# Graph network with two residual layers: one tile's sums over edges gathered by transfers instead of multiplied, in steps two to twelve

## The chip, the cores and the metric

One core of a Trainium2 chip runs the whole program. The metric is the device time of one execution in microseconds; a time given for a kernel is the median of its runs.

## What is computed

A graph of 3125 nodes with 128 features and 53125 edges `(src, dst)`, sorted by `dst`, among them a loop at each node. Two residual layers; the first has twelve steps:

```python
def L0(h, src, dst):                     # h = relu(layernorm(x))
    h = tanh(h @ W_in + b_in)
    deg = clip(segment_sum(1, dst), 1)[:, None]
    for _ in range(12):
        agg = segment_sum(h[src], dst) / deg
        h = h + (tanh(gelu(agg @ W1 + b1) @ W2 + b2) - relu(clearance) * h) * 0.5
    return h
x = x + L0(relu(layernorm(x)), src, dst)
x = x + L1(relu(layernorm(x)), src, dst) # two GCN convolutions, loops added, normed by degree
```

In the reference's inputs no node of the tail tile (below) has more than 26 edges.

## The kernel before

**Sums over edges as products.** The kernel builds the adjacency matrix of counts, `adj`, once in SBUF as f16 (25 tiles of source nodes by 3125 destination nodes). Each step, the sum over edges is a product of TensorE: `edge_sums` multiplies, for a group of destination nodes, all 25 tiles of the state with their part of `adj`. The f32 state is split into two f16 parts, `hi` (made on ScalarE) and `lo` (made on VectorE), so that a group takes 49 products (the short last tile holds both parts in one).

**Groups.** The 25 tiles of destination nodes form seven groups, `GROUPS`: five of four tiles (512 columns), a sixth, g = 5, of 437 columns (tiles 21 to 24) and the tail, g = 6, of the one tile 20 (nodes 2560 to 2687, 128 columns). For a group PE's order in `step` is `edge_sums(g)`, `outputs(g - 2)`, `hidden(g - 1)`; behind the tail come `hidden(6)`, the first 16 products of the next step's group 0, `outputs(5)` and `outputs(6)`. `hidden` is the product with W1, `outputs` the product with W2 (one f32 product for each tile and each half of the hidden row, so eight for four tiles). VectorE has `means` (division by the degree), `add_bias`, `update` (the new state) and `lo` of the next step; ScalarE has `gelu`, `tanh` and `hi` of the next step. ScalarE starts on `hi` for the next step when the tail's sums are done, since these are the last that read the old parts. Each engine works through its own queue in the order written; semaphores hold them together. Step one, `first_step`, has its own order, steps two to eleven are a loop, and step twelve has the next layer's first work mixed in (`last_step`: `add_loops`, `add_input`, `row_factors`, `norm_rows`).

**Entry.** SyncE (SP) loads the edges; VectorE finds for windows of five destination nodes where their edges start (`thresholds`, `past`, `here`, then `start_i`), and GpSimd (POOL) fetches each window's edges by five indirect transfers (L524). Then 52 batches of windows are turned into columns of `adj`: VectorE makes one-hot rows (L1168), TensorE multiplies them (L611), ScalarE copies the result (L913). Between the batches stands the entry product: GpSimd scales the rows of x to the layer norm's (L530, 25 tiles), and TensorE transposes and multiplies them. `degrees` and a flag check that all edges were found (`missed`); with the flag set, a general path would be taken, which these inputs don't take. GpSimd has nothing to do after the entry, and the DMA little until step twelve.

Of the kernel before, what the change touches and what calls it, by code (L numbers as in the profile page):

```python
# [28 lines left out]
NODES = 3125  # L29
# [23 lines left out]
LAST_HEAD = GROUP_TILES  # L53

# [35 lines left out]
ROW_BOUND = 12.0  # L90


def gnn_kernel(nc, x, src, dst, W_in, b_in, W1, b1, W2, b2, clearance, G1, gb1, G2, gb2, out):
    ctx = ExitStack()
    with ctx:
# [12 lines left out]
        x2_dram = nc.dram_tensor("x2_scratch", (NODES, FEAT), F32).ap()  # L108
        rest_dram = nc.dram_tensor("rest_scratch", (TILES, P, NODES), F16).ap()
# [16 lines left out]
        cols = sb("cols", [128, 300], F32)  # L126
        flag = sb("flag", [1, 1], I32)
        scratch = sb("scratch", [128, SCRATCH], F32)
# [18 lines left out]
        now_unscale = col(1)  # L147
        next_scale = col(1)
        top = col(4)
# [4 lines left out]
        deg = col(TILES)  # L154
        rdeg = col(TILES)
        root = col(TILES)
        dinv = col(TILES)
        assert at[0] <= 300
        spare = cols[:, at[0] - 4 * TILES:at[0]]
        stats2 = spare[:, 0:12 * 6].rearrange("p (k s) -> p k s", s=6)  # L160
        guess = spare[:, 12 * 6:12 * 6 + TILES]
# [14 lines left out]
        assert o + 512 == SCRATCH  # L176

# [20 lines left out]
        term_rest = [late[0:terms, 9, c:c + FEAT] for c in range(1302, 1302 + 2 * FEAT, FEAT)]  # L198
        yT = [late[:, 4 * i:4 * i + 4, 1302:1302 + P] for i in range(2)]
# [36 lines left out]
        thresholds = place(WINDOWS)  # L236
        past = place(WINDOWS)
        here = place(WINDOWS)
# [14 lines left out]
        row_i = place(WINDOWS, talli)  # L253
        ones16 = place(1, tall).bitcast(F16)
# [47 lines left out]
        s_y = sem("entry_rows_ready")  # L302
        s_yT = sem("entry_rows_transposed")
# [34 lines left out]
        s_xr = [sem(f"x_reloaded{g}") for g in range(NG)]  # L338
# [3 lines left out]
        s_x2o = [sem(f"x2_stored{g}") for g in range(NG)]  # L342
# [23 lines left out]
        s_res = sem("result_stored")  # L366

# [21 lines left out]
        def _(sp):  # L389
# [21 lines left out]
            def store_norms(done):  # L411
                sp.dma_start(window_layout(rdeg_dram), rdeg[0:WQ, :].rearrange("p (g d) -> p g d", g=WCOLS)
                             ).then_inc(done, 16)
                sp.dma_start(window_layout(dinv_dram), dinv[0:WQ, :].rearrange("p (g d) -> p g d", g=WCOLS)
                             ).then_inc(done, 16)
# [7 lines left out]

            sp.wait_ge(s_norms, 1)
            store_norms(s_norms_out)
# [5 lines left out]
            with sp.If(missed != 0):  # L431
# [14 lines left out]
                sp.dma_start(deg[0:WQ, :].rearrange("p (g d) -> p g d", g=WCOLS), window_layout(deg_dram)  # L446
# [4 lines left out]
                store_norms(g_normso)  # L451
# [6 lines left out]


            for g in range(NG + 2):  # L460
                if g < NG:
                    sp.wait_ge(s_aggT, (STEPS - 1) * NG + g + 1 + OPEN)
                    for sbuf, dram in rows(xload, x, g):
                        sp.dma_start(sbuf, dram).then_inc(s_xr[g], 16)
                if g >= 2:
# [3 lines left out]
                    for sbuf, dram in rows(state, x2_dram, b):  # L469
                        sp.dma_start(dram, sbuf).then_inc(s_x2o[b], 16)  # L470
# [14 lines left out]
        def _(pool):  # L485
# [3 lines left out]
            nc.gpsimd.iota(thresholds, pattern=[[WIN, WINDOWS]], base=0, channel_multiplier=0, **big)  # L489
            nc.gpsimd.iota(chunk_d[:, CHUNK + 1:CHUNK + 2], pattern=[[0, 1]], base=0, channel_multiplier=CHUNK, **big)  # L490
            nc.gpsimd.iota(wfirst, pattern=[[WQ * WIN, WCOLS]], base=0, channel_multiplier=WIN, **big).then_inc(s_const, 1)
# [30 lines left out]
            for g in range(WCOLS):  # L522
                pool.wait_ge(s_start, g + 1)
                nc.gpsimd.indirect_dma_start(  # L524
                    wedge_i[:, g, :], None, packed_dram.rearrange("(n o) -> n o", o=1),
                    bass.IndirectOffsetOnAxis(ap=start_i[:, g:g + 1], axis=0)).then_inc(s_wedges[g], 16)
            pool.wait_ge(s_ln, 1)
            for g, (k0, nt) in enumerate(GROUPS):
                for k in range(k0, k0 + nt):
# [4 lines left out]
            missed = pool.value_load(flag[0:1, 0:1], min_val=0, max_val=1)  # L534
            with pool.If(missed != 0):
# [3 lines left out]

                def stream_rest(turn, g):  # L540
                    c0, n = SPANS[g]
                    with pool.Fori(0, TILES) as k:
                        pool.wait_ge(s_restu, (turn * NG + g) * TILES + k + OPEN)
                        pool.dma_start(rest_tile[:, 0:n],
                                       rest_dram[bass.ds(k, 1), :, c0:c0 + n].rearrange("k p d -> p (k d)")
                                       ).then_inc(s_rest[g], 16)

                with pool.Fori(0, STEPS + 2) as t:
# [5 lines left out]
        def _(pe):  # L554
# [4 lines left out]
            for g in range(WCOLS):  # L559
                nc.tensor.matmul(ps[0:WQ, g, 0:CHUNK + 2], here[:, g * WQ:(g + 1) * WQ], chunk_d, start=True, stop=True  # L560
                                 ).then_inc(s_chunk, 1)
            pe.wait_ge(s_ident, 2)
# [12 lines left out]
            def degree_total():  # L575
                pe.wait_ge(s_deg, 1)
                nc.tensor.matmul(ps[0:1, 7, 64:65], deg_sum[0:WQ, :], ones_col[0:WQ, :], start=True, stop=True
                                 ).then_inc(s_degsum, 1)


            def entry_transpose(g):
                k0, nt = GROUPS[g]
                pe.wait_ge(s_y, g + 1)
# [156 lines left out]

            pe.wait_ge(s_last[2], 1)
# [20 lines left out]
            def step(t, last):  # L762
                for g in range(NG):
                    if g == 0:
                        edge_sums(t, 0, (s_hi, s_lo), t * NG, (HEAD, TILES)).then_inc(s_agg, 1)
                    else:
                        pe.wait_ge(s_aggT, t * NG + g - 1 + OPEN)
                        edge_sums(t, g, (s_hi, s_lo), t * NG).then_inc(s_agg, 1)
                    if g >= 2:
                        outputs(t, g - 2)  # L770
                    if g >= 1:
# [82 lines left out]
        def _(act):  # L854
# [43 lines left out]

            def entry_copy(g):
# [19 lines left out]
            for b in range(ENTRY_BATCHES):  # L919
# [6 lines left out]
                if b - 1 in PROD_AT:  # L926
                    entry_tanh(PROD_AT.index(b - 1))
                    split_hi(PROD_AT.index(b - 1), PROD_AT.index(b - 1) + 1, first_scale)
            with act.Fori(ENTRY_BATCHES // 2, BATCHES // 2) as i:
# [99 lines left out]
        def _(dve):  # L1029
# [43 lines left out]

            for g in range(WCOLS):
# [6 lines left out]
                                ).then_inc(s_start, 1)  # L1081

# [42 lines left out]
            def degrees():  # L1125
# [4 lines left out]
                                     root[0:WQ, :].rearrange("p (g d) -> p g d", d=WIN), ALU.subtract))  # L1130
                V.tensor_reduce(deg_sum[0:WQ, :], deg[0:WQ, :], AX.X, ALU.add).then_inc(s_deg, 1)
# [45 lines left out]
            for b in range(ENTRY_BATCHES):  # L1177
# [8 lines left out]
                if b == 6:  # L1186
# [3 lines left out]
                    link(V.tensor_copy(total[0:1, :], ps[0:1, 7, 64:65]))  # L1190
                    V.tensor_scalar(flag[0:1, 0:1], total[0:1, :], float(EDGES), None, ALU.not_equal).then_inc(s_flag, 1)
# [10 lines left out]
            with dve.If(missed != 0):  # L1202
# [57 lines left out]
                half_, y_ = root[0:WQ, :], dinv[0:WQ, :]  # L1260
                then(V.tensor_scalar(rdeg[0:WQ, :], deg[0:WQ, :], 1.0, None, ALU.max))
                then(V.reciprocal(rdeg[0:WQ, :], rdeg[0:WQ, :]))
                then(V.tensor_scalar(deg[0:WQ, :], deg[0:WQ, :], 1.0, None, ALU.add))
                then(V.tensor_scalar(half_.bitcast(I32), deg[0:WQ, :].bitcast(I32), 1, None, ALU.arith_shift_right))
                then(V.tensor_scalar(y_.bitcast(I32), half_.bitcast(I32), -1.0, float(0x5F3759DF), ALU.mult, ALU.add))
                for _ in range(4):
                    then(V.tensor_tensor(half_, y_, y_, ALU.mult))
                    then(V.scalar_tensor_tensor(out=half_, in0=half_, scalar=-0.5, in1=deg[0:WQ, :], op0=ALU.mult,
# [5 lines left out]

            dve.wait_ge(s_last[2], 1)
# [6 lines left out]
            def means(t, g, first=False):  # L1282
# [4 lines left out]
                source = ps[:, FIRST_BANK[g], :] if first else ps_agg[2 if g == TAIL else g % 2]  # L1287
# [289 lines left out]
```

## Time and profile before

| | us |
|---|---|
| runs | 1301.18, 1301.23, 1305.0; median 1301.23 |
| the profiled execution | 1300.27 |
| its span | 1298.5 |
| TensorE busy | 1255.0 |
| VectorE / ScalarE / GpSimd busy | 400.9 / 298.3 / 64.4 |

The span is what the profile's records cover; the time of the execution lies 1.77 us above it. All rows below count from the span's start. The entry takes until some 132 us, step one until some 202 us, steps two to twelve some 86.6 us each, and the second layer the rest. The granted clock of TensorE is 1.00 in the steps, which is the 2.4 GHz level.

### The profile page before, as it was taken

How to read it: one execution, taken by the hardware profiler on the slowest of the kernel's cores; microseconds unless marked ns; L12 is line 12 of the kernel's file. 1: busy time of each engine (PE TensorE's matmuls, PEld its weight loads, DVE VectorE, ACT ScalarE, POOL GpSimd, SP SyncE). 2: the span in 40 equal slices, each digit the busy share in tenths (PEclk: the TensorE clock that was granted, in tenths of full speed). 3: DMA queues.
4: the chain of work that ended last, by engine and by line, in shares of the span. 5: the costliest groups of instructions: out<-in, count | busy, mean ns of one | idle time of the engine just before them, and what ended most of it. 6: DMA issues, size and time to landing. Idle time of an engine off the chain costs nothing.

```text
span 1298.5 us, 17275 instructions
## 1 busy us (share of the span) xinstructions
PE 1255.0 (97%) x7194; PEld 707.0 (54%) x7194; DVE 400.9 (31%) x817; ACT 298.3 (23%) x438; POOL 64.4 (5%) x56
## 2 busy tenths in 40 slices
PE   3888999999999999999999999999999999999998
PEld 1766465564565645645656456456564564565545
DVE  7999122131131221311312213113122132382312
ACT  1898221131121211311212113112121131120100
POOL 4940000000000000000000000000000000000000
PEclk7899999999999999999999999999999999999999
DMA  3000200000000000000000000000000000220101
GB/s 100 3 1 2 63 1 1 1 1 0 0 0 0 0 0 0 0 0 0 0 0 0 0 0 0 0 0 0 0 0 0 0 1 24 66 61 1 50 17 34
DMA packets 24552, 13.77 MB, mean 11 GB/s; under 512 B 6173, under 2 KB 23609, under 8 KB 24388
## 3 DMA queue, kind: packets, MB, share of 16 engines
q1 hardware_dynamic: 22334, 11.88, 3.4%
q10 hardware_dynamic: 1782, 1.06, 0.3%
q8 instruction: 26, 0.43, 0.1%
q0 software_dynamic: 400, 0.33, 0.1%
q14 instruction: 10, 0.08, 0.0%
HBM read 9.42 MB, written 3.44 MB: 10 GB/s over the span
## 4 chain that ended last, share of the span: by engine, by line
PE 88%; DVE 8%; issue 2%; DMA 1%; ACT 0%; DVEq 0%; SPq 0%; POOL 0%; ACTq 0%; POOLq 0%
PE ps L715 63%; PE ps L757 10%; PE ps L748 9%; DVE scratch L1168 5%; PE ps L628 3%; PE ps L829 1%; DVE lo L1151 1%; DMA adj<-packed_scratch,adj 1%; PE ps L611 0%; PE ps L571 0%; DVE cols L1367 0%; DMA adj<-in_dst_dram 0%; DVE state L1394 0%; PE ps L565 0%; DVE ps L1295 0%
## 5 line engine op out<-in xcount | busy, mean ns | idle before, releaser
L715 PE MATMUL ps<-adj,hi 128*128 128x512 f16 (+2 forms) x2275 | 747.2, 352 | 1.3 <-DVE lo L1151 1.3
L715 PE MATMUL ps<-adj,lo 128*128 128x512 f16 (+2 forms) x2184 | 730.4, 351 | 0.0
L715 PEld LDWEIGHTS ps<-adj,hi 128*128 128x128 f16 x2275 | 220.8, 97 | 228.0 <-issue 14.5
L715 PEld LDWEIGHTS ps<-adj,lo 128*128 128x128 f16 x2184 | 212.4, 97 | 224.1 <-issue 18.2
L1295 DVE TENSOR_TENSOR ps<-ps,bias 128x512 f32<-128x512 f32 (+1 forms) x84 | 53.9, 641 | 532.4 <-PE ps L757 532.4
L955 ACT ACTIVATE scratch<-ps 128x512 f32<-128x512 f32 (+1 forms) x84 | 46.3, 552 | 614.7 <-DVE ps L1295 614.6
L946 ACT ACTIVATE scratch<-ps,b1c,cols 128x512 f32<-128x512 f32 (+2 forms) x168 | 111.9, 724 | 170.7 <-PE ps L748 169.9
L757 PEld LDWEIGHTS ps<-w,scratch 128*128 128x128 f32 x1200 | 144.2, 192 | 8.1
L757 PE MATMUL ps<-w,scratch 128*128 128x128 f32 x1200 | 146.1, 275 | 0.0
L748 PE MATMUL ps<-scratch,w 128*128 128x512 f32 (+2 forms) x336 | 137.8, 538 | 0.0
L1288 DVE TENSOR_TENSOR scratch<-ps,scratch 128x512 f32<-128x512 f32 (+2 forms) x84 | 51.9, 619 | 178.7 <-PE ps L748 131.3
L1168 DVE TENSOR_TENSOR scratch<-scratch 128x1536 f16<-128x1536 f16 (+1 forms) x106 | 92.2, 940 | 0.5 <-PE ps L611 0.5
L913 ACT ACTIVATE adj<-ps 128x1500 f16<-128x1500 f32 (+1 forms) x52 | 76.0, 1480 | 14.9 <-PE ps L611 14.6
L748 PEld LDWEIGHTS ps<-scratch,w 128*128 128x128 f32 x336 | 57.3, 191 | 38.9 <-issue 37.2
L1300 DVE SCALAR_TENSOR_TENSOR state<-state,cols,scratch 128x512 f32<-128x512 f32 (+1 forms) x84 | 58.3, 694 | 47.0 <-ACT scratch L955 46.7
L611 PE MATMUL ps<-scratch 128*128 128x125 f16 x625 | 55.4, 249 | 13.2 <-DVE scratch L1168 11.9
L1151 DVE SCALAR_TENSOR_TENSOR lo<-state,cols,hi 128x512 f16<-128x512 f32 (+2 forms) x91 | 59.9, 672 | 13.6 <-ACT hi L857 12.8
L611 PEld LDWEIGHTS ps<-scratch 128*128 128x128 f16 x625 | 45.8, 110 | 29.0 <-DVE scratch L1168 25.7
L628 PE MATMUL ps<-adj,hi 128*128 128x512 f16 (+2 forms) x175 | 58.8, 353 | 1.6 <-ACT adj L933 1.6
L628 PE MATMUL ps<-adj,lo 128*128 128x512 f16 (+2 forms) x168 | 56.6, 352 | 0.0
L857 ACT ACTIVATE hi<-state,cols 128x512 f16<-128x512 f32 (+1 forms) x84 | 52.1, 669 | 19.4 <-PE ps L715 17.3
L530 POOL TENSOR_SCALAR state<-state,cols 128x128 f32<-128x128 f32 x25 | 49.2, 1981 | 11.4 <-DVE cols L1139 11.4
(143 smaller groups left out, 247.7 us busy)
## 6 DMA issues: line engine op xcount, KB each, us to landing
scratch<-rdeg_scratch SPq DMA_DIRECT2D x1, 1562.5 KB, 8.8
state<-in_x_dram SPq DMA_DIRECT2D x5, 256.0 KB, 3.7
scratch<-in_x_dram SPq DMA_DIRECT2D x5, 256.0 KB, 2.7
x_scratch<-state SPq DMA_DIRECT2D x5, 256.0 KB, 2.7
scratch<-dinv_scratch SPq DMA_DIRECT2D x5, 256.0 KB, 3.9
state<-x_scratch SPq DMA_DIRECT2D x5, 256.0 KB, 3.1
out_dram<-state SPq DMA_DIRECT2D x5, 256.0 KB
adj<-adj ACTq DMA_DIRECT2D x1, 390.6 KB, 9.1
```

The source lines that it names most:

```text
L611: return nc.tensor.matmul(target[:, :, place * WIN:(place + 1) * WIN], Lb[buf][:, b, :, i_], Rb[buf][:, b, :, i_].rearrange("p (k d) -> p ...
L628: mm = nc.tensor.matmul(ps[:, FIRST_BANK[g], 0:n], values[:, k, :], adj[:, k, c0:c0 + n], start=(at == 0 and values is hi), stop=(k == SHORT))
L715: return nc.tensor.matmul(bank, values[:, k, :], adj[:, k, c0:c0 + n], start=is_first, stop=is_last)
L748: nc.tensor.matmul(ps_hid_tail[h] if g == TAIL else ps_hid[h][:, 0:n], w1[:, h * FEAT:(h + 1) * FEAT], agg[g == TAIL][:, 0:n], start=True, ...
L757: mm = nc.tensor.matmul(ps_out[g == TAIL][:, i * FEAT:(i + 1) * FEAT], hid[g == TAIL][:, h, i * P:(i + 1) * P], w2[:, h, :], start=(h == 0 ...
L857: nc.scalar.activation(tiles_of(hi, group), tiles_of(state, group), ACT.Copy, scale=factor).then_inc(s_hi, 1)
L913: nc.scalar.activation(adj[:, :, bass.ds((i * 2 + u) * BATCH * WIN, BATCH * WIN)].rearrange("p k (b c) -> p b k c", b=BANKS), ps[:, 3 * u: ...
L946: nc.scalar.activation(hid[g == TAIL][:, h, 0:n], ps_hid_tail[h] if g == TAIL else ps_hid[h][:, 0:n], ACT.Gelu, bias=b1c[:, h:h + 1], scal ...
L1151: return V.scalar_tensor_tensor(out=lo[:, k0:k1, :], in0=values[:, k0:k1, :], scalar=0.0 if factor is None else factor, in1=hi[:, k0:k1, : ...
L1168: last_ = V.tensor_tensor(buf[:, 0:b, :, 0:w], c_.broadcast_to((128, b, m, w)), k_.broadcast_to((128, b, m, w)), ALU.is_equal)
L1295: V.tensor_tensor(p_, p_, bias_of(1, nt), ALU.add).then_inc(s_bias, 1)
L1300: V.scalar_tensor_tensor(out=tiles_of(state, g), in0=tiles_of(state, g), scalar=now_keep, in1=act_out[:, 0:n_], op0=ALU.mult, op1=ALU.add) ...
```

## The change

**The tail's sums.** In steps two to twelve the sums over edges of the tail tile are no longer multiplied. After each step, SP stores the new f32 state to `state_dram` (3125 rows and a row of zeros). GpSimd then gathers: for c = 0 to 31, one indirect transfer brings to each of 128 partitions the row of the c-th edge of its node, or the row of zeros where the node has fewer edges. Three tiles in SBUF take them in turn (`tail_sum`, rooms that are free in the steps): the first transfer to a tile overwrites, the others add (`compute_op`), and each waits until the one before it into the same tile has landed. TensorE adds the three by products with the identity (`tail_sums`), which also transposes. As these sums are of unscaled rows, `means` multiplies the tail by a scale of the step.

**The list of rows.** `tail_rows` (128x32) comes from one more search in the entry: 128 more columns in `thresholds`, `past` and `here`, one more product, four operations on VectorE, one more indirect transfer, and five small operations on GpSimd. If a node had more than 32 edges, or others were missing, all rows would point to the zeros and the old products would run.

**The order in group g = 5.** Its sums are cut at place 15 (`SPLIT`); `hidden(4)` and `outputs(3)` stand between the two parts, in this order.

**Rows of x.** The first two groups (eight tiles) are scaled on ScalarE instead of GpSimd. The small degree vectors move from `cols` to room in `adj`; `s_xr` and `s_x2o` are merged into other semaphores.

```diff
+ACT_ROWS = 2
+
+CAP = 32
+TAIL_NODE = GROUPS[TAIL][0] * P
+PLACES = 3
+PLACE_TURNS = [len(range(i, CAP, PLACES)) for i in range(PLACES)]
...
+        tail_sum = [w_in[:, :], bias[:, 0, :], hid[1][:, 0, :]][0:PLACES]
...
-        thresholds = place(WINDOWS)
-        past = place(WINDOWS)
-        here = place(WINDOWS)
+        thresholds = place(WINDOWS + P)
+        past = place(WINDOWS + P)
+        here = place(WINDOWS + P)
...
+            def store_state(t):
+                for g in range(NG):
+                    sp.wait_ge(s_upd, t * NG + g + 1)
+                    for sbuf, dram in rows(state, state_dram, g):
+                        sp.dma_start(dram, sbuf).then_inc(s_st[g], 16)
+
+            store_state(1)
+            with sp.Fori(2, STEPS) as t:
+                for i in range(PLACES):
+                    sp.wait_ge(s_place[i], t * (16 * PLACE_TURNS[i]) - 16 * PLACE_TURNS[i])
+                store_state(t)
...
+            pool.wait_ge(s_start, WCOLS + 1)
+            nc.gpsimd.indirect_dma_start(
+                tail_rows[:, :], None, packed_dram.rearrange("(n o) -> n o", o=1),
+                bass.IndirectOffsetOnAxis(ap=tail_start, axis=0)).then_inc(s_tedge, 16)
+            nc.gpsimd.memset(tail_block[:, 0:WIN], 0.0)
+            pool.wait_ge(s_tedge, 16)
+            nc.gpsimd.tensor_scalar(tail_f, tail_rows[:, :], tail_base, None, ALU.subtract).then_inc(s_tc2, 1)
+            pool.wait_ge(s_tc2, 1)
...
+                if g < ACT_ROWS:
+                    continue
...
+            pool.wait_ge(s_mrow, 1)
+            nc.gpsimd.tensor_scalar(tail_rows[:, :], tail_f, missing_row, None, ALU.max).then_inc(s_trow, 1)
...
+            def gather_tail(t):
+                for g in range(NG):
+                    pool.wait_ge(s_st[g], t * (16 * parts(g)))
+                for c in range(CAP):
+                    i, turn = c % PLACES, c // PLACES
+                    before = (t - 1) * PLACE_TURNS[i] + turn
+                    if before:
+                        pool.wait_ge(s_place[i], 16 * before)
+                    nc.gpsimd.indirect_dma_start(
+                        tail_sum[i], None, state_dram, bass.IndirectOffsetOnAxis(ap=tail_rows[:, c:c + 1], axis=0),
+                        compute_op=ALU.bypass if turn == 0 else ALU.add).then_inc(s_place[i], 16)
...
+            for t in range(1, STEPS):
+                gather_tail(t)
+                with pool.If(missed != 0):
+                    for g in range(NG):
+                        stream_rest(t, g)
...
+            def tail_sums(t):
+                bank = ps_agg[2][:, 0:P]
+
+                def place(i):
+                    pe.wait_ge(s_place[i], t * (16 * PLACE_TURNS[i]))
+                    return nc.tensor.matmul(bank, tail_sum[i], ident[:, :], start=(i == 0), stop=(i == PLACES - 1))
+
+                for i in range(PLACES - 1):
+                    place(i)
+                with pe.If(missed != 0):
+                    for k in range(TILES):
+                        c0, n = SPANS[TAIL]
+                        nc.tensor.matmul(bank, hi[:, k, :], adj[:, k, c0:c0 + n], start=False, stop=False)
+                        if k != SHORT:
+                            nc.tensor.matmul(bank, lo[:, k, :], adj[:, k, c0:c0 + n], start=False, stop=False)
+                    with pe.Fori(0, TILES) as r:
+                        add_rest(t, TAIL, bank, r)
+                return place(PLACES - 1)
...
+                        if g == TAIL:
+                            tail_sums(t).then_inc(s_agg, 1)
+                        elif g == TAIL - 1:
+                            edge_sums(t, g, (s_hi, s_lo), t * NG, (0, SPLIT))
+                            hidden(t, g - 1)
+                            outputs(t, g - 2)
+                            edge_sums(t, g, (s_hi, s_lo), t * NG, (SPLIT, TILES)).then_inc(s_agg, 1)
+                        else:
+                            edge_sums(t, g, (s_hi, s_lo), t * NG).then_inc(s_agg, 1)
+                    if g >= 2 and g != TAIL - 1:
                         outputs(t, g - 2)
-                    if g >= 1:
+                    if g >= 1 and g != TAIL - 1:
...
+            act.wait_ge(s_ln, 1)
+            for g in range(ACT_ROWS):
+                k0, nt = GROUPS[g]
+                for k in range(k0, k0 + nt):
+                    last = nc.scalar.activation(state[:, k, :], state[:, k, :], ACT.Identity, bias=ln_b[:, k:k + 1],
+                                                scale=ln_a[:, k:k + 1])
+                last.then_inc(s_ya, 1)
...
+            V.tensor_scalar(tail_base, tail_first, float(PACK), None, ALU.mult)
...
+            dve.wait_ge(s_chunk, WCOLS + 1)
+            link(V.tensor_scalar(tail_junk, ps[:, WCOLS, 0:CHUNK], tail_first, 0.0, ALU.is_lt, ALU.add,
+                                 accum_out=tail_found))
+            link(V.tensor_scalar(tail_start_f, tail_found, ps[:, WCOLS, CHUNK + 1:CHUNK + 2], 0.0, ALU.add, ALU.max))
+            V.tensor_scalar(tail_start, tail_start_f, float(EDGES - CAP), None, ALU.min).then_inc(s_start, 1)
...
+                V.tensor_tensor(tail_block[0:WQ, 0:WIN], deg[0:WQ, w0:w0 + WIN], tail_mask, ALU.mult)
...
-                    link(V.tensor_copy(total[0:1, :], ps[0:1, 7, 64:65]))
-                    V.tensor_scalar(flag[0:1, 0:1], total[0:1, :], float(EDGES), None, ALU.not_equal).then_inc(s_flag, 1)
+                    V.tensor_scalar(total, ps[:, 7, 64:65], float(EDGES), None, ALU.not_equal)
+                    link(V.tensor_reduce(missing, ps[:, 7, 96:96 + WIN + CAP], AX.X, ALU.add))
+                    link(V.scalar_tensor_tensor(out=missing, in0=missing, scalar=0.0, in1=total, op0=ALU.not_equal,
+                                                op1=ALU.max))
+                    V.tensor_scalar(flag[0:1, 0:1], missing[0:1, :], 0.0, None, ALU.add).then_inc(s_flag, 1)
+                    V.tensor_scalar(missing_row, missing, float(NODES), None, ALU.mult).then_inc(s_mrow, 1)
...
+                if g == TAIL and not first:
+                    V.scalar_tensor_tensor(out=agg[1], in0=source[:, 0:n_], scalar=now_tail, in1=row[:, c0:c0 + n_],
+                                           op0=ALU.mult, op1=ALU.mult).then_inc(s_aggT, 1)
+                    return
...
+                if not isinstance(t, int) or t > 0:
+                    dve.wait_ge(s_st[g], t * (16 * parts(g)))
...
+                V.tensor_scalar(now_tail, tail_scale[:, bass.ds(t, 1)], 1.0, None, ALU.mult)
```

## Rows read from the trace of the kernel before

**Rows 1.** The page, part 1: busy time, share, instructions.

```profile
PE 1255.0 (97%) x7194; PEld 707.0 (54%) x7194; DVE 400.9 (31%) x817; ACT 298.3 (23%) x438; POOL 64.4 (5%) x56
```

**Rows 2.** The chain that ended last, 345 to 378 us: start, us, what.

```profile
349.81 9.09 PE ps L715 x49
358.90 1.78 PE ps L757 x16
360.68 1.72 PE ps L748 x4
362.40 2.76 PE ps L715 x49
365.16 1.84 PE ps L757 x16
367.00 1.91 PE ps L748 x8
368.92 3.46 PE ps L715 x16
```

**Rows 3.** The same chain over the whole span.

```profile
12.84 7.36 DMA adj<-packed_scratch,adj
...
448.97 2.76 PE ps L715 x49
...
1128.91 9.08 PE ps L715 x49
...
1167.90 4.05 PE ps L715 x18
```

**Rows 4.** POOL's instructions in order of time, 12 to 20 us.

```profile
14.55 1.21 POOL L524 DMA_INDIRECT adj<-packed_scratch,adj  x1 [0.31 <-issue]
16.06 1.21 POOL L524 DMA_INDIRECT adj<-packed_scratch,adj  x1 [0.30 <-issue]
```

**Rows 5.** One line's instructions, L524: landing.

```profile
DMA to landing us min/median/max: 3.1/3.4/3.6
```

**Rows 6.** DVE in order of time, 374 to 378 us.

```profile
376.95 0.35 DVE L1300 SCALAR_TENSOR_TENSOR state<-state,cols,scratch 128x128 f32<-128x128 f32 x1 [0.42 <-ACT scratch L955]
```

**Rows 7.** One line's instructions, L470: SP's stores of x2 rows.

```profile
L470 SPq DMA_DIRECT2D x_scratch<-state x8: 320/364/374, 1103.0 to 1161.7; - x8
...
DMA to landing us min/median/max: 1.6/2.6/3.9
```

**Rows 8.** All engines in order of time, 360.6 to 363.5 us.

```profile
360.72 0.70 DVE L1295 TENSOR_TENSOR ps<-ps,bias 128x512 f32<-128x512 f32 x1 [9.79 <-PE ps L757]
...
362.03 1.44 ACT L946 ACTIVATE scratch<-ps,b1c,cols 128x512 f32<-128x512 f32 x2
...
362.83 0.61 DVE L1288 TENSOR_TENSOR scratch<-ps,scratch 128x437 f32<-128x437 f32 x1
```

**Rows 9.** Windows: busy us by engine, PEclk, DMA share, GB/s.

```profile
12.00:20.00 8.00, 3.23 (x7) 1.25 (x5) 5.53 (x24) 1.49 (x2) 5.94 (x5) 0.84 0.90 220
30.00:82.00 52.00, 44.98 (x432) 37.30 (x433) 51.32 (x73) 43.68 (x42) 49.18 (x25) 0.89 0.06 2
380.00:449.00 69.00, 69.00 (x342) 35.62 (x340) 8.51 (x13) 8.26 (x13) 0.00 (x0) 1.00 0.00 0
```

(The engines stand in the order PE, PEld, DVE, ACT, POOL.)

**Rows 10.** Groups by line and form: busy us, mean ns, idle before.

```profile
L530 POOL TENSOR_SCALAR state<-state,cols 128x128 f32<-128x128 f32 x25 | 49.2, 1981 | 11.4 <-DVE cols L1139 11.4
...
L955 ACT ACTIVATE scratch<-ps 128x128 f32<-128x128 f32 x12 | 3.3, 278 | 15.7 <-DVE ps L1295 15.7
...
L1312 DVE TENSOR_SCALAR cols<-cols 128x1 f32 x10 | 1.5, 154 | 0.0
```

**Rows 11.** DVE in order of time, 4 to 21 us.

```profile
7.94 0.87 DVE L1052 SCALAR_TENSOR_TENSOR adj<-adj 125x625 f32<-125x625 f32 x1
...
20.22 0.29 DVE L1100 TENSOR_SCALAR adj<-adj 125x128 f32<-125x128 int32 x1 [1.98 <-DMA adj<-packed_scratch,adj]
```

**Rows 12.** DVE in order of time, 1138 to 1142 us.

```profile
1141.85 0.61 DVE L1288 TENSOR_TENSOR scratch<-ps,scratch 128x437 f32<-128x437 f32 x1
```

More of the change, by code:

```diff
@@ L53 @@
 LAST_HEAD = GROUP_TILES
+SPLIT = TILES - 10
 WIN = 5
@@ L147, in gnn_kernel @@
         now_unscale = col(1)
+        missing = col(1)
+        missing_row = col(1)
+        now_tail = col(1)
         next_scale = col(1)
+        tail_scale = bound
         top = col(4)
@@ L153, in gnn_kernel @@
         dinv_col = col(TILES)
[L154 to L161, printed above, removed]
+        guess = col(TILES)
+        stats2 = col(GROUP_TILES * 6).rearrange("p (k s) -> p k s", s=6)
+        assert at[0] <= 252
         row = scratch[:, 0:NODES]
@@ L198, in gnn_kernel @@
         term_rest = [late[0:terms, 9, c:c + FEAT] for c in range(1302, 1302 + 2 * FEAT, FEAT)]
+        deg, rdeg, root, dinv = (late[:, 7, 1440 + i * TILES:1440 + (i + 1) * TILES] for i in range(4))
+        general_deg, general_rdeg, general_root, general_dinv = (act_out[0:WQ, i * TILES:(i + 1) * TILES]
+                                                                 for i in range(4))
+        tail_f, tail_neg, tail_block = (late[:, 4, 1440:1440 + CAP], late[:, 5, 1440:1440 + CAP],
+                                        late[:, 6, 1440:1440 + WIN + CAP])
+        tail_mask = late[0:WQ, 6, 1500:1500 + WIN]
         yT = [late[:, 4 * i:4 * i + 4, 1302:1302 + P] for i in range(2)]
@@ L253, in gnn_kernel @@
         row_i = place(WINDOWS, talli)
+        tail_first, tail_base, tail_found, tail_start_f = (place(1, tall) for _ in range(4))
+        tail_start = place(1, talli)
+        tail_junk = place(CHUNK, tall)
         ones16 = place(1, tall).bitcast(F16)
@@ L366, in gnn_kernel @@
         s_res = sem("result_stored")
+        s_zero = sem("zero_row_stored")
+        s_tedge = sem("tail_edges_loaded")
+        s_tc2 = sem("tail_rows_chain")
+        s_tmask = sem("tail_mask_ready")
+        s_mrow = sem("missing_row_ready")
+        s_trow = sem("tail_rows_ready")
+        s_tab2 = sem("tail_scales_ready")
+        s_place = [sem(f"tail_rows_added{i}") for i in range(PLACES)]
+        s_st = [sem(f"state_stored{g}") for g in range(NG)]
         block = ctx.enter_context(nc.Block())
@@ L538, in _ @@
                 pool.wait_ge(g_pair, 16)
[L540 to L548, printed above, removed]
+                for g in range(NG):
+                    stream_rest(0, g)
+            pool.wait_ge(s_trow, 1)
+            pool.wait_ge(s_zero, 16)
+            for t in range(1, STEPS):
+                gather_tail(t)
+                with pool.If(missed != 0):
+                    for g in range(NG):
+                        stream_rest(t, g)
+            with pool.If(missed != 0):
+                with pool.Fori(STEPS, STEPS + 2) as t:
                     for g in range(NG):
@@ L561, in _ @@
                                  ).then_inc(s_chunk, 1)
+            nc.tensor.matmul(ps[:, WCOLS, 0:CHUNK + 2], here[:, WINDOWS:], chunk_d, start=True, stop=True
+                             ).then_inc(s_chunk, 1)
             pe.wait_ge(s_ident, 2)
@@ L1267, in _ @@
                     then(V.tensor_tensor(half_, y_, y_, ALU.mult))
-                    then(V.scalar_tensor_tensor(out=half_, in0=half_, scalar=-0.5, in1=deg[0:WQ, :], op0=ALU.mult,
+                    then(V.scalar_tensor_tensor(out=half_, in0=half_, scalar=-0.5, in1=general_deg, op0=ALU.mult,
                                                 op1=ALU.mult))
@@ L1358, in add_input @@
                 dve.wait_ge(s_upd, STEPS * NG + g + 1)
-                dve.wait_ge(s_xr[g], 16 * parts(g))
+                dve.wait_ge(s_x[g], 2 * 16 * parts(g))
                 if k1 < k0 + nt:
```

94 lines of the change are left out of this document (69 added, 25 removed).

## The prediction, made before the changed kernel ran

> **What bounds the kernel now.** I read the page first: TensorE is busy for 1255.0 of 1298.5 us [rows 1]. Then the chain that ended last, over one step of the loop. Its pieces touch each other and all belong to PE [rows 2], and the same place of the next step, the sums of the tail, comes 448.97 - 362.40 = 86.57 us later [rows 2, 3]. So a step costs what PE has to do in it, and PE's work that is taken out comes out of the time, unless something else becomes late. The reader is to see in [rows 2]: the sixth group's sums (x49, 9.09 us), the outputs of group 3 (1.78), the hidden product of group 4 (1.72), the tail's sums (x49, 2.76), the outputs of group 4 (1.84), the hidden products of groups 5 and 6 (1.91), then the next step's first sums. Outside the steps, the entry stage is another kernel: there DVE is busy for 51.32 of 52 us [rows 9]. In the last step DVE takes over too: from 1141.85 us [rows 12] the chain runs over it until the next layer's sums start at 1167.90 [rows 3].
>
> **The tail's sums, the term that pays.** Steps two to twelve lose 49 products of 128 columns, 2.76 us each time [rows 2]. In their place stand three f32 products of 128x128 with the identity. An outputs turn has eight such products, shows as 16 records and takes 1.78 us [rows 2], so three are 6 records x 0.111 = 0.67 us. Saving per step 2.76 - 0.67 = 2.09 us. The branch on the flag was inside the tail's sums before and stays; formerly 49 short products hid it, now two do. I take 0 for it and keep up to 0.5 us a step for the range (the whole new group is 0.67).
>
> **The order in the sixth group.** 30 of its 49 products (15 tiles) run first, then hidden(4), outputs(3), then 19 products, the tail, outputs(4). Nothing is added on PE; the question is only whether outputs(4) finds gelu(4) done. In the trace of before outputs(3) ends at 360.68, the bias starts at 360.72, and after it and tanh the two gelus run from 362.03 to 363.47 [rows 2, 8]: 2.79 us after the outputs. After the change PE has 19 x 9.09/49 = 3.52 plus 0.67 = 4.19 us between. Covered, with 1.4 us to spare; had hidden(4) and outputs(3) stayed behind the sums, only 1.72 + 0.67 us would lie there and each step would stall by about 0.4 us. means(5) (0.61 us [rows 8]) has the tail's 0.67 and outputs(4)'s 1.78 us as cover before hidden(5). After the tail everything stands as before, since the high parts of the next step wait for the tail's sums in both kernels. So I count 2.09 us in a step of the loop.
>
> **The gather, which has to be hidden.** A step's gather is 32 indirect transfers of 128 rows of 512 B on POOL, in three accumulators; a transfer waits for the landing of the one three before it. It starts when the new state lies in DRAM. The last update ends at 376.95 + 0.35 = 377.30 [rows 6]; SP then issues the last store (0.36 us), and eight like it land after 1.6 to 3.9, median 2.6 us [rows 7]. That is 379.3 to 381.6, by the median 380.3; as the last one is a single tile, I take 380.0. PE comes to the tail at 448.97 [rows 3], no later after the change than before, counted from there. Cover: 69.0 us.
> The nearest rows are the five indirect loads of window edges, 125 rows of 512 B: 16.06 - 14.55 = 1.51 us from issue to issue, and 3.1 to 3.6 us from issue to landing; the first took 7.36 us until it was used, beside a DMA that moved 220 GB/s [rows 3 to 5, 9]. By issue the gather takes 31 x 1.51 + 3.4 = 50.2 us. By landing it takes 11 rounds of 3.4 = 37.4 us. Neither row adds to its destination. An adding one must read the sum first; if that costs as much again as the shortest landing of a store, a round is 3.4 + 1.6 = 5.0 us, 55.0 us in all. I take 50 to 55, hidden by 14 us or more, so its price on PE is 0. Bounds of a round: 3.1 below and 7.36 above.
> If the gather takes G, a step is G + (86.57 - 2.09 - 69.0) = G + 15.5 us. It starts to cost at G = 69.0 (a round of 6.27 us, or an issue every 2.12) and is slower than before from G = 71.1, a round of 6.46 us.
> DVE and POOL can hinder one another: POOL's row scaling took 1981 ns for a 128x128 tile while DVE had no pause [rows 9, 10], and DVE is busy for 8.51 us between 380 and 449 [rows 9]. Were every one of them lost to POOL, G would be 59 to 64, still covered.
> [...]
>
> **Queues.** SP gets 8 stores a step, 88 in all, and waits for the former gather before it stores the next state; behind that wait stand only stores, and x's reloads in the last step, which wait for the first means of that step anyway. update() newly waits for the store of the former state, some 20 us older than its place. POOL has nothing else to do in the steps. One more tiny DVE operation in step_scales (0.15 us [rows 10]) falls into DVE's idle time.
>
> **The last step.** There DVE is the bound. means(5) starts at 1141.85 in before [rows 12], after the update of group 3. After the change the sixth group ends at 1128.91 [rows 3] + 12.59 (9.09, 1.78 and 1.72) = 1141.50, and means(5) can start some 0.2 later, at 1141.70. DVE's chain behind it is unchanged, so this step gives 0.15 us, not 2.09.
>
> **Entry.** x's first two groups go to ACT: eight tiles at 278 ns (the row of a 128x128 tanh [rows 10]) = 2.2 us, and ACT is busy for 43.68 of 52 us there [rows 9], so 0. POOL's 25 tiles fill 49.2 us [rows 10], the 17 left over 33.7; the chain holds none of them, so nothing is won either. DVE, the bound, gets more: `past` and `here` grow from 625 to 753 columns (0.87 us [rows 11] x 0.20, twice: 0.35), and five small operations come in (tail_base, one product in degrees(), three at the flag) at 0.15 us [rows 10], some 0.2 with their waits, another 1.0: about 1.3 us. The search of the tail's edges, four operations as for each window group, falls into the 1.98 us for which DVE waits for the first window edges [rows 11], and so may part of the first terms. I take +1.0, bounds 0 and 3.
>
> **Sum.** 10 x 2.09 + 0.15 = 21.05 off, 1.0 on: 20.05. The profiled execution took 1300.27 us, so 1280.2. The median of the runs lies 0.96 above it: 1281.2, forecast **1281 us**.
>
> **Rivals.**
> *The gather comes late* (slower, one mechanism: an adding round on POOL is longer than 6.46 us). For it: no row shows an adding transfer, one traced transfer took 7.36 us, and twice the 3.4 would be 6.8. Against it: the 7.36 was beside some 220 GB/s of loads, and in the steps the DMA is idle [rows 9]. Price: with 6.8 us, G = 74.8, a step 90.3, 3.7 us more than now, x11 = 41: about 1343 us. With 7.36, G = 81.0, a step 96.5: about 1411. Were the issue to double to 3.0 us (twice as many descriptors), G = 96: about 1570. Chance 0.16 for slower, and 0.03 that it falls between 6.3 and 6.5 us and there is no change.
> *PE stalls at the small tail group* (branch, three waits, gelu late): up to 0.8 us a step, 8 us in all, 1285 to 1290. For it: three products hide little. Against it: 1.4 us spare in the hand-over. Chance 0.12.
> *The whole gain is hidden, because DVE or ACT sets the step*: against it, DVE and ACT are busy 8.51 and 8.26 of 69 us [rows 9]. Chance 0.01.
> *The change doesn't do what it says*: if a node of the tail had over 32 edges, the rows would all point to the zero row and the old sums would run again. In the reference's inputs its nodes have at most 26. Chance under 0.01.
> *The forecast*: chance 0.68, own range 1277 to 1286.
>
> **Numbers that follow.** Faster 0.80, same 0.04, slower 0.16; 0.3% (4 us) is about what a measurement of this kernel can tell from no change. The range takes the forecast and the stall: from 1275 (all eleven steps at 2.09 and nothing for the entry is 1278, less 3 for what the rows can't resolve) to 1294 (0.5 us a step for the branch, 3 for the entry, and the start of a late gather). What is left out is the late gather.
>
> **What would show it.** Tail group on PE: 6 records, 0.67 us, step 84.5 us, no PE idle before it: right. A wait of PE for a DMA into w_in, bias or hid at the tail: late gather. 352 adding transfers on POOL, their distance 1.5 to 1.7 us and last landing 50 to 55 us after the first: right; distance above 2.1: wrong. outputs(4) waiting for ACT: the stall. In the last step means(5) moves by under 0.3 us relative to its group's start. The first step's sums start 1 us later than before.

## The result, and the profile after

The changed kernel takes 1280.6 us (median of four runs, 1279.38 to 1281.51) against 1301.2 before: ratio 0.984, interval 0.9828 to 0.9852, some 20.6 us less. The forecast was 1281 us, range 1275 to 1294.

The chain that ended last, over the same step of the changed kernel (start, us, what). L819 are the sums over edges, L871 hidden, L880 outputs, L850 the three products with the identity:

```profile
348.89 5.56 PE ps L819 x30
354.46 1.72 PE ps L871 x4
356.17 1.78 PE ps L880 x16
357.96 3.52 PE ps L819 x19
361.48 0.67 PE ps L850 x6
362.15 1.79 PE ps L880 x16
363.94 1.91 PE ps L871 x8
365.85 3.46 PE ps L819 x16
```

Beside [rows 2]: the 2.76 us of the tail are 0.67, in six records, and nothing stands between the pieces. The outputs behind them come again at 446.57 (whole chain), 84.42 us after 362.15; a step took 86.57. From that whole chain, the places where the other parts show:

```profile
133.27 14.67 PE ps L732 x67
...
446.57 1.79 PE ps L880 x16
...
1108.67 5.56 PE ps L819 x30
...
1147.40 4.05 PE ps L819 x18
```

From the sixth group to the next layer's sums the last step takes 38.73 us, 38.99 before [rows 3]: it gains 0.26. The first step's sums start at 133.27; before, at 132.04 by the same chain. The balance of the span: 10 x 2.15 = 21.5 and 0.26 off, 1.23 on, 20.5; the span went from 1298.5 to 1278.1, by 20.4.

The gather (L627), POOL in order of time in that step (each bracket: idle before, and what ended it):

```profile
293.67 1.00 POOL L627 DMA_INDIRECT w_in<-state_scratch,tail_rows  x1 [27.18 <-DMA state_scratch<-state]
294.97 0.96 POOL L627 DMA_INDIRECT bias<-state_scratch,tail_rows  x1 [0.30 <-issue]
...
297.50 1.57 POOL L627 DMA_INDIRECT w_in<-state_scratch,tail_rows  x1 [0.30 <-issue]
299.37 1.55 POOL L627 DMA_INDIRECT bias<-state_scratch,tail_rows  x1 [0.31 <-issue]
...
349.43 1.55 POOL L627 DMA_INDIRECT bias<-state_scratch,tail_rows  x1 [0.31 <-issue]
```

Three overwriting transfers at 1.25 to 1.30 us apart, then adding ones at 1.85, and in this step never a wait for a landing: POOL's issue sets the pace. The last one is issued at 349.43, 55.8 us after the first; PE comes to the tail at 361.48. The cover is 361.48 - 293.67 = 67.8 us. Ten of the eleven gathers take 55.7 to 56.1 us from first to last issue. The last one takes 57.5 us, with the only two waits for a landing (1.17 and 0.30 us).

### The profile page after: what moved, and what is told of

Read it like the earlier page. It is cut to its first block, busy times and chain, and to the rows that moved or that the text cites. A ratio compares the mean times of both kernels' runs of the same rounds, so it can differ in the third digit from the quotient of the medians.

```text
span 1278.1 us, 17094 instructions
## 1 busy us (share of the span) xinstructions
PE 1234.4 (97%) x6725; PEld 688.0 (54%) x6725; DVE 406.4 (32%) x840; ACT 301.1 (24%) x446; POOL 572.4 (45%) x413
## 4 chain that ended last, share of the span: by engine, by line
PE 88%; DVE 7%; issue 2%; DMA 1%; ACT 1%; DVEq 0%; SPq 0%; POOL 0%; ACTq 0%; POOLq 0%
PE ps L819 62%; PE ps L880 10%; PE ps L871 10%; DVE scratch L1319 4%; PE ps L732 3%; PE ps L960 1%; PE ps L715 1%; PE ps L850 1%; DMA adj<-packed_scratch,adj 1%; DVE lo L1302 0%; PE ps L670 0%; DMA adj<-in_dst_dram 0%; DVE adj L1188 0%; DVE state L1560 0%; PE ps L664 0%
## 5 line engine op out<-in xcount | busy, mean ns | idle before, releaser
L819 PE MATMUL ps<-adj,hi 128*128 128x512 f16 (+2 forms) x2000 | 715.7, 370 | 2.0 <-DVE lo L1302 2.0
L819 PE MATMUL ps<-adj,lo 128*128 128x512 f16 (+2 forms) x1920 | 698.9, 370 | 0.0
L627 POOL DMA_INDIRECT w_in<-state_scratch,tail_rows x121 | 181.9, 1504 | 455.0 <-DMA state_scratch<-state 393.0
L819 PEld LDWEIGHTS ps<-adj,hi 128*128 128x128 f16 x2000 | 194.6, 97 | 225.1 <-issue 12.6
L819 PEld LDWEIGHTS ps<-adj,lo 128*128 128x128 f16 x1920 | 186.7, 97 | 219.6 <-issue 14.6
L627 POOL DMA_INDIRECT bias<-state_scratch,tail_rows x121 | 181.6, 1501 | 37.8 <-issue 36.6
L627 POOL DMA_INDIRECT scratch<-state_scratch,tail_rows x110 | 164.0, 1491 | 33.6 <-issue 33.3
L880 PEld LDWEIGHTS ps<-w,scratch 128*128 128x128 f32 x1200 | 144.2, 192 | 13.3 <-issue 5.3
L880 PE MATMUL ps<-w,scratch 128*128 128x128 f32 x1200 | 145.7, 275 | 0.6 <-ACT scratch L1087 0.6
L871 PE MATMUL ps<-scratch,w 128*128 128x512 f32 (+2 forms) x336 | 138.0, 538 | 0.0
L1449 DVE TENSOR_TENSOR scratch<-ps,scratch 128x512 f32<-128x512 f32 (+2 forms) x73 | 48.8, 670 | 172.4 <-PE ps L871 131.3
L871 PEld LDWEIGHTS ps<-scratch,w 128*128 128x128 f32 x336 | 58.0, 190 | 40.3 <-issue 36.9
L732 PE MATMUL ps<-adj,hi 128*128 128x512 f16 (+2 forms) x175 | 58.8, 353 | 1.6 <-ACT adj L1074 1.6
```

The costliest lines, as they stand in the source:

```text
L627: nc.gpsimd.indirect_dma_start(tail_sum[i], None, state_dram, bass.IndirectOffsetOnAxis(ap=tail_rows[:, c:c + 1], axis=0), compute_op=ALU. ...
L732: mm = nc.tensor.matmul(ps[:, FIRST_BANK[g], 0:n], values[:, k, :], adj[:, k, c0:c0 + n], start=(at == 0 and values is hi), stop=(k == SHORT))
L819: return nc.tensor.matmul(bank, values[:, k, :], adj[:, k, c0:c0 + n], start=is_first, stop=is_last)
L871: nc.tensor.matmul(ps_hid_tail[h] if g == TAIL else ps_hid[h][:, 0:n], w1[:, h * FEAT:(h + 1) * FEAT], agg[g == TAIL][:, 0:n], start=True, ...
L880: mm = nc.tensor.matmul(ps_out[g == TAIL][:, i * FEAT:(i + 1) * FEAT], hid[g == TAIL][:, h, i * P:(i + 1) * P], w2[:, h, :], start=(h == 0 ...
```

## The experiments

All are edits of the changed kernel but e2, which is an edit of the one before. Times are medians; e4 and e12 are single executions.

**e1, the old order in the sixth group.**

```diff
-                        elif g == TAIL - 1:
-                            edge_sums(t, g, (s_hi, s_lo), t * NG, (0, SPLIT))
-                            hidden(t, g - 1)
-                            outputs(t, g - 2)
-                            edge_sums(t, g, (s_hi, s_lo), t * NG, (SPLIT, TILES)).then_inc(s_agg, 1)
...
-                    if g >= 2 and g != TAIL - 1:
+                    if g >= 2:
...
-                    if g >= 1 and g != TAIL - 1:
+                    if g >= 1:
```

> The changed kernel with the sixth group's sums in one piece again (sums, outputs of group 3, hidden product of group 4, tail, outputs of group 4). Theory: only the hidden product (1.72) and the small tail group (0.67) lie between the outputs of group 3 and those of group 4, and gelu of group 4 is done 2.79 us after the former, so PE waits 0.4 us a step for ACT; step 84.8 instead of 84.42, about 1285 us. Rival (the cut does nothing): 1280.6 us, no wait of the outputs' matmuls on ACT.

1289.2 us, ratio 0.9907 (0.9892 to 0.9922); a step takes 85.22 us (452.68 to 537.90 in its chain). All engines in order of time, behind the tail:

```profile
447.22 1.44 ACT L1082 ACTIVATE scratch<-ps,b1c,cols 128x512 f32<-128x512 f32 x2
...
447.78 0.39 PE L850 MATMUL ps<-ident,scratch 128*128 128x128 f32 x2
...
448.71 2.05 PE L880 MATMUL ps<-w,scratch 128*128 128x128 f32 x16 [0.54 <-ACT scratch L1082]
```

L1082 is gelu here. PE waits 0.54 us for it, and the same outputs then take 2.05 us instead of 1.79, another 0.26. The granted clock stays 1.00 in the steps, so the clock is not the reason. Their first weight load starts with them at 448.71, while in the changed kernel it starts 0.11 us ahead of the products (361.88 and 361.99); that this makes the 0.26 is not shown. The theory stands, its price was half of the measured 0.80 us a step.

**e2, the new order without the gather.** The same cut in the kernel before.

> The kernel before with only the new order in the sixth group. Theory: there the tail's 2.76 us already cover gelu of group 4, so nothing is to be had: step 86.57, 1301 us, within 0.3 us in the last step. Rival (the order gives a part of the gain by itself): step below 86.4, 1299 us or less.

1301.1 us, ratio 0.9996 (0.9987 to 1.0005). The cut is worth nothing by itself; once the tail is short it keeps 8.6 of the 20.6 us (1289.2 against 1280.6).

**e3, both: gather and products.** (`means` also divides the tail as before; that line is left out here.)

```diff
-                for i in range(PLACES - 1):
-                    place(i)
...
-                return place(PLACES - 1)
+                for i in range(PLACES):
+                    pe.wait_ge(s_place[i], t * (16 * PLACE_TURNS[i]))
+                return edge_sums(t, TAIL, (s_hi, s_lo), t * NG)
```

> The changed kernel with all stores and gathers running, but the tail's sums multiplied as before from the f16 parts; the gathered rows are waited for and not used. Theory: gather and stores cost PE nothing, all the gain is in the replaced products; step 86.5, and the entry's 1.2 us on top of before: 1302 to 1303 us. Rival (44 GB/s of traffic and POOL's 48 us a step slow DVE, ACT or PE somewhere): step above 86.8, over 1305 us.

1303.0 us, ratio 1.0008 (0.9999 to 1.0017); the sums of group 0 come at 456.65 and 543.22, a step of 86.57 us as before. 88 stores and 352 indirect transfers (11 gathers of 32) cost the step nothing that shows. So the gain is the replaced products, with the order that lets them count (e1).

**e4, one accumulator** (`PLACES = 1`).

> PLACES 1: all 32 transfers of a step go into one accumulator, each waits for the landing of the one before. A step is then the gather plus 16.6 us, so its length gives the round of an adding transfer, which no row shows. Theory (round 5.0 us, the value taken in the prediction): step 177 us, about 2300 us. Rival, landing as in the loads of before (3.4): step 125, about 1730 us. Rival, twice that (6.8): step 234, about 2930 us.

1940 us. POOL in order of time, two transfers late in one gather and one early in the next:

```profile
306.67 1.55 POOL L627 DMA_INDIRECT w_in<-state_scratch,tail_rows  x1 [2.89 <-DMA w_in<-state_scratch,tail_rows]
311.08 1.55 POOL L627 DMA_INDIRECT w_in<-state_scratch,tail_rows  x1 [2.87 <-DMA w_in<-state_scratch,tail_rows]
...
362.56 1.56 POOL L627 DMA_INDIRECT w_in<-state_scratch,tail_rows  x1 [2.00 <-DMA w_in<-state_scratch,tail_rows]
```

A round of adding takes 4.41 us late in a gather (311.08 - 306.67), of which the transfer is 4.15 in the chain, and 3.5 us early in one. The mean over the eleven gathers is 3.93 us, between the 3.4 of the loads and the 5.0 that the prediction took. POOL's part of an adding transfer is 1.55 us from the first to the last of them, by median. The wait behind it is 2.0 us until the 14th transfer, rises until about the 25th and stays at 2.9 (medians by place). From the 27th on all 128 partitions take the row of zeros, since no node has more than 26 edges, and before that more and more of them do. That reading one row so often slows the landing would fit, but no run here isolates it.

**e12, one accumulator and no adding** (`compute_op=ALU.bypass` for all; the tail's sums are left out, only the last row arrives).

> PLACES 1 as in e4, but no transfer adds, all 32 overwrite (the sums of the tail are left out: only the last row arrives). e4 gave 4.15 us from issue to landing and 1.55 us on POOL for an adding transfer. Theory (adding costs POOL 0.6 us in making the descriptors and nothing behind it): on POOL 0.95 us, landing 3.5 to 3.6 us, about 1750 us. Rival (the read of the destination also takes time behind POOL): landing under 3.3 us, under 1700 us. Rival (adding costs nothing but issue overlaps): landing 4.1 as in e4, 1930 us.

1703 us. The same view, again late and early:

```profile
304.64 0.94 POOL L627 DMA_INDIRECT w_in<-state_scratch,tail_rows  x1 [2.99 <-DMA w_in<-state_scratch,tail_rows]
308.52 0.94 POOL L627 DMA_INDIRECT w_in<-state_scratch,tail_rows  x1 [2.93 <-DMA w_in<-state_scratch,tail_rows]
...
339.48 0.94 POOL L627 DMA_INDIRECT w_in<-state_scratch,tail_rows  x1 [1.83 <-DMA w_in<-state_scratch,tail_rows]
```

0.94 us on POOL instead of 1.55. The wait behind it is 2.9 us in both late in a gather, 1.8 against 2.0 early, and 2.30 against 2.40 in the mean. So adding costs 0.68 us a round (3.93 against 3.25 in the mean): 0.6 on POOL and 0.1 behind it. The theory stands for that split. Its 1750 us came out too high because it took e4's 4.15, a landing late in a gather, for every transfer; that the total came near the 1700 of the rival with time behind POOL is luck, since that time is only 0.1 us.

**e5, two accumulators** (`PLACES = 2`).

> PLACES 2: 16 rounds in two accumulators. Issue alone takes 31 x 1.85 = 57 us, which 67.8 us cover. Theory: it stays hidden if a round is below (67.8 - 2) / 16 = about 4.2 us, then 1281 us; with a round of 5.0 the gather takes 80 us, a step 96.6, about 1415 us. Between, the time rises by 16 x 11 = 176 us for each us of round above 4.2.

1280.9 us, ratio 0.9849 (0.9834 to 0.9864). Two issues take 3.7 us, more than a round early in a gather (3.5) and less than one late in it (4.4), so POOL now waits in the later half; in the same step the transfers start from 292.55 to 354.93, 62.4 us instead of 55.8, and with a landing of 4.15 the gather ends 1.3 us before PE's 360.35. Two would have done, but only just.

**e6 and e7, 36 and 40 transfers a step** (`CAP`).

> CAP 36: four more transfers a step, 36 in all. By issue 35 x 1.85 - 3 x 0.55 = 63.1 us, plus a landing of 3 to 5 us: 66 to 68, just under the 67.8 us of cover. Theory (bound by POOL's issue): 1281 us, up to 4 us more. Rival (landings set the pace, and the gather is nearer to its cover than the issue shows): 1290 us and more.

> CAP 40: by issue 39 x 1.85 - 3 x 0.55 = 70.5 us plus 3 to 5 us of landing, so 74 to 75.5, over the cover by 6 to 8 us; a step is gather + 16.6 = 90.5 to 92.1. Theory: 1348 to 1366 us, with PE waiting before the tail. Rival (something else than the tail's wait follows the gather, or it has more cover than counted): under 1330.

CAP 36: 1280.1 us, ratio 0.9839 (0.9824 to 0.9854); the last issue is at 356.88, its landing by e4's 4.15 at 361.0, and PE reaches the tail at 361.55. CAP 40: 1385.8 us, ratio 1.0646 (1.063 to 1.0662). The whole loss comes with four more transfers. In its chain:

```profile
468.94 4.41 DMA w_in<-state_scratch,tail_rows
473.39 1.65 PE ps L850 x6
475.04 2.69 PE ps L880 x16
477.74 1.91 PE ps L871 x8
```

The gather starts at 398.39 and ends at 473.35, 75.0 us, as worked out. The step is 473.39 - 378.65 = 94.7 us and not 91.6. Its windows (length, busy us of PE, PEld, DVE, ACT, POOL, then PEclk, DMA share, GB/s) say why:

```profile
360.00:370.00 10.00, 10.00 (x57) 6.03 (x55) 1.17 (x3) 1.06 (x3) 8.48 (x6) 1.00 0.30 36
370.70:378.60 7.90, 1.01 (x6) 0.32 (x4) 0.61 (x1) 0.37 (x1) 4.64 (x3) 0.74 0.30 34
378.65:386.10 7.45, 7.45 (x31) 6.43 (x32) 3.44 (x6) 4.16 (x7) 0.00 (x0) 0.60 0.51 141
```

The products of the tail in PE's rows, with the wait before them:

```profile
378.65 0.80 PE L850 MATMUL ps<-ident,w_in 128*128 128x128 f32 x2 [6.93 <-DMA w_in<-state_scratch,tail_rows]
```

PE waits 6.93 us for the last transfer. In the windows shown its granted clock is 0.74 during that wait and 0.60 behind it; narrower ones give 0.50, the 1.2 GHz level, from 375.00 to 384.60, and 1.00 from 386.15. The tail, the outputs and the hidden products take 7.51 us from 378.65 instead of 4.37 (0.67, 1.79, 1.91). These 3.1 us are the difference between 94.7 and 91.6. The step shown loses 94.7 - 84.4 = 10.3 us, the mean of the eleven steps is 9.6 (105.2 by 11).

**e8, all rows of x on POOL** (`ACT_ROWS = 0`).

> ACT_ROWS 0: POOL scales all 25 tiles of x again. Theory: POOL was not on the path of the entry, ACT neither; within 1 us of 1280.6. Rival (the eight tiles on ACT are worth something, or cost something, in the entry): the first step's sums start more than 1 us later or earlier than at 133.3 us.

1280.4 us, ratio 0.9841 (0.9828 to 0.9854): no difference. Its profiled execution starts the first sums at 135.38, over 1 us later, which was the rival's sign; but it ran at another clock of PE in the entry, and e10 at the same clock needs as long with the rows on ACT (table below). So the eight tiles are worth nothing that shows.

**e9, the mask's operations behind POOL's iotas.**

```diff
-            nc.gpsimd.memset(tail_mask, 1.0).then_inc(s_tmask, 1)
...
             nc.gpsimd.iota(count_r.rearrange("p (k d) w -> p k d w", d=WIN), pattern=[[1, TILES], [LANES, WIN], [0, RUN]],
                            base=1, channel_multiplier=0, **big).then_inc(s_counts, 1)
+            nc.gpsimd.memset(tail_mask, 1.0).then_inc(s_tmask, 1)
...
```

> The tail mask's three small POOL operations are issued behind the two large iotas (counts) instead of ahead of them. In the trace of the changed kernel DVE's cast of the destinations (1.45 us before, 2.58 now) ends 0.24 us after POOL's last large iota, as in the kernel before. Theory (the cast waits for that iota, and what POOL does ahead of it delays it): the iotas end some 0.6 us earlier, the cast too, first step's sums 0.6 us earlier, 1280 us. Rival (the wider search, past and here, sets the start of the window transfers): no change in the cast's end relative to them, 1280.6.

**e10 and e11, the iotas behind the bias chain, or behind the five window transfers.**

> Both large iotas go behind POOL's chain on the bias (b_in), ahead of the window transfers. Theory: DVE's cast has no iota beside it and takes about 0.3 us instead of 2.58; the search starts 2 us earlier; what of it arrives depends on the landing of the first window transfer beside x's loads: 1278 to 1279.6 us. Rival (the iotas now delay other DVE operations or the transfers themselves): the same 1280.6, or later.

> The same iotas behind the five window transfers. Theory: the cast takes about 0.3 us, the transfers start about 2 us earlier; the iotas then stand beside the key operations on DVE (L1247, L1253), which may wait for up to 1.9 us. 1278 to 1280.6 us, by which of the two weighs more.

1279.5 us (ratio 0.9832, 0.9819 to 0.9846), 1279.4 (0.9823, 0.9808 to 0.9839) and 1281.0 (0.9838, 0.9825 to 0.9852). First DVE's cast of the destinations (L1188) and POOL's last large iota, in the changed kernel, DVE's row and then POOL's:

```profile
5.03 2.58 DVE L1188 CAST adj<-adj 125x426 f32<-125x426 int32 x1
```

```profile
5.47 1.90 POOL L556 IOTA scratch<- 128x250 f16 x1
```

and the cast in e10, with no iota beside it:

```profile
5.17 0.38 DVE L1188 CAST adj<-adj 125x426 f32<-125x426 int32 x1
```

The same operation, 2.58 or 0.38 us. With the iota it ends 0.24 us after the iota does (7.37 and 7.61); in e9, with the iotas 0.58 us earlier, it takes 1.73 and ends at 7.02. e11 shows the other side: its iotas stand beside a key operation (L1247), which takes 1.89 us instead of 0.28.

How much of this reaches the steps is harder to read, since single profiles differ in the entry. The start of one-hot work, the start of the first sums, the time between them, and the granted clock of PE from 50 to 60 us:

| run | one-hot | first sums | between | PEclk |
|---|---|---|---|---|
| before | 29.32 | 132.04 | 102.7 | 1.00 |
| e2 (entry of before) | 30.02 | 132.73 | 102.7 | 1.00 |
| changed | 30.29 | 133.27 | 103.0 | 0.83 |
| e1, e3, e5 (entry as changed) | 30.54, 30.73, 29.83 | 133.03, 133.21, 132.36 | 102.5 | 1.00 |
| e6 (entry as changed) | 30.50 | 133.34 | 102.8 | 0.83 |
| e8 | 30.70 | 135.38 | 104.7 | 0.66 |
| e9 | 29.73 | 132.26 | 102.5 | 1.00 |
| e10 | 28.35 | 133.02 | 104.7 | 0.66 |
| e11 | 30.59 | 133.57 | 103.0 | 0.83 |

(e7, with the low clock from 40 to 50 us instead, has 103.6.) So the time between goes with the clock, and at 1.00 it is no longer with the change than without. One-hot work starts 0.9 us apart in runs with the same entry (29.83 to 30.73, and 31.93 in e4). e9's first sums at 132.26 are therefore no proof for moving the mask: e5, where the mask stands as in the changed kernel, has them at 132.36. What e9 shows is the cast and the first window transfer 0.6 to 0.7 us earlier (13.30 against 14.01 for the transfer). Windows of the entry, 50 to 60 us, of e9 and then of e10:

```profile
50.00:60.00 10.00, 8.50 (x90) 7.02 (x87) 10.00 (x13) 9.97 (x11) 10.00 (x5) 1.00 0.18 3
```

```profile
50.00:60.00 10.00, 9.44 (x75) 8.63 (x76) 8.30 (x11) 8.67 (x10) 4.37 (x4) 0.66 0.17 1
```

At 0.66 DVE has pauses (8.30 us busy instead of 10.00) while PE is busy for 9.44 us, and e10's start, 2 us earlier, is gone again at 133.02. At like clock it isn't: e8, also at 0.66, has its first sums at 135.38, 2.4 us later. e10's executions too are some 2 us faster than the changed kernel's at like mean clock: 1276.79 and 1277.64 against 1279.38 and 1279.68 us at 0.990 to 0.991, and 1279.36 and 1279.41 against twice 1281.51 at 0.987. That is a hint and no more: neither e9 nor e10 can be told from the changed kernel by their intervals.

## Why the prediction was right

**The tail's products.** Right: 0.67 us in six records, and the branch costs nothing. A step saves 2.15 us instead of 2.09, since the outputs behind the tail take 1.79 instead of 1.84. The late-branch rival (1285 to 1290) falls.

**The order.** Right that gelu is covered: in the changed kernel ACT ends it at 360.84 and PE wants it at 362.15, 1.3 us to spare of the 1.4 forecast. e1 shows the price without it, 0.80 us a step; the 0.4 of the text became a wait of 0.54, and left out the 0.26 by which the outputs behind it are longer.

**The gather is hidden.** Right, with less room than forecast. Three sizes were off. It starts 3.8 us after the last update (289.91 to 293.67), not 2.7; the wait is for SP's last stores, which land after 2.3 to 3.1 us. Adding transfers come every 1.85 us, not 1.51. A landing late in the gather takes 4.15 us from issue (e4), where 3.4 to 5.0 was written. Together 55.8 + 4.15 = 59.9 us of 67.8, 7.9 us to spare instead of 14 or more. The pace was that of POOL's issue, as the lower of the two estimates had it; landings begin to set it with two accumulators (e5). The prediction's own signs don't decide it: they named a distance of 1.5 to 1.7 us and a last landing after 50 to 55 us as right, and a distance above 2.1 as wrong. Its 352 adding transfers are 319, for 33 of the 352 overwrite.

**The late gather** was the right rival, and e6 and e7 put its edge between 36 and 40 transfers. Its price was too low: the formula (gather plus a constant, with the measured 16.6 us for it) gives 91.6 us for a step of 94.7, because after the wait of 7 us TensorE worked on at the lower clock.

**The last step.** Right in kind, 0.26 us instead of 0.15: DVE bounds it, and the shorter tail is lost there. `means(5)` starts at 1121.30, 12.63 us behind its group's start, instead of 12.94 [rows 3, 12].

**Entry.** The sum was near (1.23 between the two profiled executions, 1.0 forecast), the mechanism wrong. The step that failed is "DVE, the bound, gets more: `past` and `here` grow ... and five small operations come in", with 1.0 of its 1.3 us for the small operations. In its place the traces show three things.

First, new small work on POOL pushed its iotas back, and DVE's cast waits for them: it ends at 7.61 instead of 6.65, 0.96 us that the prediction did not have, and that repeats (6.64 in e2, 7.59 to 7.61 in all runs with that part of the entry unchanged).

Second, the wider `past` and `here` take 0.20 us more in the chain (0.71 and 1.00 against 0.64 and 0.87), where 0.35 was written. With these the first window transfer starts at 14.01 instead of 12.84.

Third, behind the start of one-hot work the small operations cost nothing that shows: 102.5 us to the first sums at clock 1.00, against 102.7 before.

Of the 1.23 between the two profiles, 0.97 lies ahead of one-hot work, whose start varies by 0.9 us and more with the same entry, and 0.26 behind it, where the changed kernel's profile has the lower clock. So 1.23 is no sharp number, and that 1.0 came so near is luck.

The Trainium skill's page "SBUF — State Buffer" (Who interferes with whom) says that a cast in a two-port mode and GpSimd shut each other out for a whole instruction; e9 to e11 agree, though no run shows in which mode this cast ran. In the gathers, where the prediction allowed for 8.5 us of such loss, next to none shows: ten of eleven keep to 55.7 to 56.1 us.

What stays open: what sets the entry's lower clock. The moved work is not needed for it: the kernel before shows the same spread, 1299.64 us at a mean clock of 0.991 to 1303.48 at 0.986 in its 21 executions beside e1 to e4. Whether the change makes the lower clock more frequent, no run isolates.

## What to carry to other kernels

An engine that idles can take a part of the bound engine's work if it fits under what is left, but count the fit from the slowest term: issue, landing of the stores it reads, and landing of the last transfer. When a group of work gets short, look at what it had covered: here 8.6 of 20.6 us would have gone without the reordering. When a wait of several us appears in front of TensorE, add the slower clock after it to its length: 3.1 us behind 6.93 here, while e1's waits of 0.54 us left the clock at 1.00. And before a difference of 1 us between two single profiles is given a cause, look how far other runs with the same code differ there.

## What the hardware showed that I had not expected

An adding indirect transfer of 128 rows of 512 B costs POOL 1.55 us against 0.94 for an overwriting one, and only 0.1 us more behind that. The landing of such a transfer is not constant: the wait behind POOL's part grows from 1.8 to 2.9 us along a gather without adding, where more and more partitions take the same row (the cause is not isolated). A cast of 426 elements on 125 partitions takes 0.38 us alone and up to 2.58 beside large iotas on POOL. TensorE's granted clock fell to 0.50 within a wait of 7 us and stayed there for another 6 us of work behind it.
